# Weighing attention probabilities in fp32 on TensorE, straight from one exponential

## The reference, cut to what matters

```python
def _attn(q, k, v, scale):
    scores = jnp.einsum('bld,bmd->blm', q, k) / scale
    w = jax.nn.softmax(scores, axis=-1)
    return jnp.einsum('blm,bmd->bld', w, v)
...
ecg_out = qkv_ecg_inter + alpha * qkv_ecg_intra
pcg_out = qkv_pcg_inter + gamma * qkv_pcg_intra
...
x_norm = _ln(x, norm_g, norm_b)
xin = jnp.einsum('bsd,hd->sbh', x_norm, W_in)
def res_step(prev, xt):
    new = jnp.tanh(xt + prev @ W_res.T)
    new = LEAK * new + (1.0 - LEAK) * prev
    return (new, new)
...
gate = jax.nn.sigmoid(x @ W_gate.T + b_gate)
return reservoir_out * gate + ssm_out * (1.0 - gate)
```

## Time and profile before

| | before |
|---|---|
| median of three runs | 626.57 us |
| span of the profiled execution | 624.1 us |
| between that span and the median | 2.5 us |
| PE busy | 587.2 us, 94% |
| DVE busy | 531.1 us, 85% |
| ACT busy | 453.6 us, 73% |
| POOL busy | 191.2 us, 31% |
| granted PE clock, mean | 0.996 |

### The profile page before, as it was taken

How to read it: one execution, slowest core, us unless ns; L and a number is a source line. 1 busy time by engine, 2 the same in 40 slices (tenths; PEclk the granted TensorE clock), 3 DMA queues, 4 the chain that set the end, 5 groups by cost and what they waited for, 6 DMA issues and landing times.

```text
span 624.1 us, 28185 instructions
## 1 busy us (share of the span) xinstructions
PE 587.2 (94%) x11015; PEld 464.1 (74%) x11015; DVE 531.1 (85%) x2335; ACT 453.6 (73%) x2244; POOL 191.2 (31%) x427
## 2 busy tenths in 40 slices
PE   7887888999999999999999999999999999999973
PEld 2554454788888788888888888888799888888762
DVE  5789997899888888888898899898767788999985
ACT  4687796677777777777777777777757677777664
POOL 1545365000000000010000000000100588888886
PEclk9999999999999999999999999999999999999998
DMA  6000000000000000000000000000030000000001
GB/s 215 2 2 1 2 1 2 4 3 4 4 3 4 4 3 4 4 4 4 3 4 4 4 3 3 4 4 4 9 64 3 3 20 19 16 16 19 15 20 30
DMA packets 8629, 8.30 MB, mean 13 GB/s; under 512 B 944, under 2 KB 7088, under 8 KB 8496
## 3 DMA queue, kind: packets, MB, share of 16 engines
q1 hardware_dynamic: 8208, 5.51, 3.2%
q10 hardware_dynamic: 288, 0.99, 0.6%
HBM read 3.35 MB, written 2.10 MB: 9 GB/s over the span
## 4 chain that ended last, share of the span: by engine, by line
PE 76%; DVE 9%; issue 5%; POOL 4%; ACT 4%; DMA 1%; POOLq 0%; SPq 0%; DVEq 0%
PE PS L1454 28%; PE PS L1501 16%; PE PS L1656 6%; PE PS L1472 4%; PE PS L1466 2%; PE PS L1461 2%; PE PS L1403 2%; PE PS L1404 2%; PE PS L1410 2%; PE PS L1634 2%; PE PS L1339 2%; PE PS L1378 2%; PE PS L1362 1%; PE PS L1645 1%; PE PS L1390 1%
## 5 line engine op out<-in xcount | busy, mean ns | idle before, releaser
L613 ACT ACTIVATE y<-PS 128x16 f16<-128x16 f32 x512 | 99.0, 193 | 128.0 <-PE PS L1466 124.3
L1501 PE MATMUL PS<-ballast,ident 128*128 128x245 f16 (+6 forms) x661 | 152.0, 300 | 0.0
L1013 DVE TENSOR_TENSOR y_lo<-ys,y 128x16 f16<-128x16 f32 x512 | 98.2, 192 | 52.9 <-ACT ys L614 40.8
L1454 PEld LDWEIGHTS PS<-y,res_hi 128*128 128x128 f16 x2048 | 97.7, 96 | 52.6 <-ACT y L613 19.0
L1454 PE MATMUL PS<-y_lo,res_hi 128*128 128x8 f16 x2048 | 128.2, 168 | 0.0
L1454 PE MATMUL PS<-y,res_hi 128*128 128x8 f16 x2048 | 127.7, 168 | 0.1
L1454 PE MATMUL PS<-y,res_lo 128*128 128x8 f16 x2048 | 123.4, 166 | 0.0
L444 POOL TENSOR_TENSOR small<-small,minus_half 128x2 f32<-128x2 f32 x32 | 22.6, 706 | 304.3 <-DVE y_lo L1013 272.1
L614 ACT ACTIVATE ys<-PS 128x16 f32<-128x16 f32 x512 | 103.8, 203 | 0.0
L575 ACT ACTIVATE prob<-PS,exp_up,sc 128x512 f32<-128x512 f32 x128 | 102.3, 806 | 1.5 <-PE PS L1390 1.3
L580 ACT ACTIVATE prob_hi<-PS,exp_up,sc 128x512 f16<-128x512 f32 x128 | 103.1, 812 | 0.0
(11 more groups left out here) (225 smaller groups left out, 1368.9 us busy)
## 6 DMA issues: line engine op xcount, KB each, us to landing
ys<-in_x SPq DMA_DIRECT2D x8, 256.0 KB, 8.0
out<-gate_all SPq DMA_DIRECT2D x24, 64.0 KB, 1.5
mats<-in_mats ACTq DMA_DIRECT2D x1, 709.0 KB, 5.1
h_last<-h_all SPq DMA_DIRECT2D x4, 128.0 KB, 3.2
gate_last<-gate_all SPq DMA_DIRECT2D x4, 128.0 KB, 2.7
out<-gate_last SPq DMA_DIRECT2D x16, 32.0 KB, 1.9
rows<-in_rows ACTq DMA_DIRECT2D x1, 257.5 KB, 8.0
wall<-in_wall SPq DMA_DIRECT2D x1, 256.0 KB, 4.8
```

The costliest lines, as they stand in the source:

```text
L613: a_.activation(y16[:, :].rearrange("p (m b) -> p m b", m=NH), pre, ACT.Tanh, scale=back).then_inc(y16_ready, 1)
L1013: v.tensor_tensor(y_lo[:, :], ys[:, :, bass.ds(i * STEPS + (1 + t), 1)].rearrange("p n o -> p (n o)"), y16[:, :], ALU.subtract).then_inc(l ...
L1454: t_.matmul(dst[:, m, :], wts[:, k, m * P:m * P + P], st[:, k * B:k * B + B], start=False, stop=False, skip_group_check=True)
L1501: t_.matmul(at[:, 0:size], ident16[:, :], ballast[:, 0:size], start=False, stop=True, skip_group_check=True)
```

## The change

The probabilities stay in fp32 and the values too: one exponential for each a (`weights_of`), no high and low parts, no `low_part`, no DVE step for the values (`stack` is for queries and keys only), and no batch scale in them, so that `mix_s` goes. `weigh` takes the place of `weigh_high` and `weigh_low`: sixteen fp32 matmuls a tile with 65 columns (64 values and the ones). It is spread over seven steps by a table; the steps of other work are set anew. The fp16 low parts of the product that were left out before are now contained in the fp32 operands.

```diff
-PV = C + 2
-VW = PV + C
+PV = C + 1
...
+        WEIGHTS_AT = (8, 9, 11, 13)
+        WEIGH_AT = {10: (0, 2), 11: (2, 4), 12: (4, 6), 13: (6, 9), 14: (9, 11), 15: (11, 13), 16: (13, 16)}
...
-                g.tensor_tensor(prob_lo[:, a, :], prob[:, a, :], prob_hi[:, a, :], ALU.subtract).then_inc(prob_lo_ready, 1)
...
-                    a_.activation(v1, PS[:, n % 2, :].rearrange("p (a c) -> p a c", c=C), ACT.Identity, scale=s_col[:, b:b + 1]
-                                  ).then_inc(rounded_ready, 1)
+                    a_.activation(v1, PS[:, n % 2, :].rearrange("p (a c) -> p a c", c=C), ACT.Copy).then_inc(valued, 1)
...
-                a_.activation(prob[:, a, :], X[a], ACT.Exp, scale=e_col[:, j % B:j % B + 1], bias=exp_up[:, :])
-
-            def high_part(j, a):
-                if j > 0:
                     act.wait_ge(pv_done, (j - 1) * NA + a + 1)
-                a_.activation(prob_hi[:, a, :], X[a], ACT.Exp, scale=e_col[:, j % B:j % B + 1], bias=exp_up[:, :]).then_inc(prob_ready, 1)
+                a_.activation(prob[:, a, :], X[a], ACT.Exp, scale=e_col[:, j % B:j % B + 1], bias=exp_up[:, :]).then_inc(prob_ready, 1)
...
+                if p in WEIGHTS_AT:
+                    weights_of(j, WEIGHTS_AT.index(p))
                 if p == 22:
                     heads(j)
-                if p == (30 if j == NT - 1 else 32) and j >= AHEAD - 1:
+                if p == (31 if j == NT - 1 else 43) and j >= AHEAD - 1:
                     gate_tanh(j)
-                if p == (31 if j == NT - 1 else 35) and j >= AHEAD - 1:
+                if p == (31 if j == NT - 1 else 45) and j >= AHEAD - 1:
                     gate_half(j)
...
-                else:
-                    vals = values[:, b * NQ + 2 * (k - 2):b * NQ + 2 * (k - 2) + 2, :, :].rearrange("p n a w -> p (n a) w")
-                    v.scalar_tensor_tensor(vals[:, :, PV:VW], PS[:, n_ % 2, :].rearrange("p (a c) -> p a c", c=C), s_col[:, b:b + 1],
-                                           vals[:, :, 0:C], ALU.mult, ALU.subtract).then_inc(stacked, 1)
...
-                if p == 21:
+                if p == 16:
...
-                a = of_a(p, 10, 2)
-                if a is not None:
-                    low_part(j, a)
-                if p == 22:
+                if p == 23:
                     head_sums(j)
-                if p == 23:
+                if p == 24:
                     moments(j)
-                if p == 25:
+                if p == 26:
                     hat(j)
-                if p == 27:
+                if p == 28:
...
-            def weigh_high(j, a):
+            def weigh(j, first, last):
                 b = j % B
-                pe.wait_ge(prob_ready, j * NA + a + 1)
-                if j > 0 and a == 0:
-                    pe.wait_ge(h_ready, j)
-                if j < B:
-                    pe.wait_ge(stacked, b * 4 + 4)
-                for k in range(NQ):
-                    lhs, vals = prob_hi[:, a, k * P:k * P + P], values[:, b * NQ + k, a, :]
-                    t_.matmul(OUT[:, a, :], lhs, vals[:, 0:PV], start=a == 0 and k == 0, stop=False, skip_group_check=True)
-                    t_.matmul(OUT[:, a, 0:C], lhs, vals[:, PV:VW], start=False, stop=False, skip_group_check=True)
-
-            def weigh_low(j, a):
-                b = j % B
-                pe.wait_ge(prob_lo_ready, j * NA + a + 1)
-                for k in range(NQ):
-                    last = t_.matmul(OUT[:, a, :], prob_lo[:, a, k * P:k * P + P], values[:, b * NQ + k, a, 0:PV], start=False,
-                                     stop=a == NA - 1 and k == NQ - 1, skip_group_check=True)
-                last.then_inc(pv_done, 1)
+                for n in range(first, last):
+                    a, k = n // NQ, n % NQ
+                    if k == 0:
+                        pe.wait_ge(prob_ready, j * NA + a + 1)
+                    if n == 0 and j > 0:
+                        pe.wait_ge(h_ready, j)
+                    if n == 0 and j < B:
+                        pe.wait_ge(const_ready, 3)
+                    if n % (2 * NQ) == 0 and j < B:
+                        pe.wait_ge(valued, 2 * b + 2)
+                    one = t_.matmul(OUT[:, a, :], prob[:, a, k * P:k * P + P], values[:, b * NQ + k, a, :], start=n == 0,
+                                    stop=n == NA * NQ - 1, skip_group_check=True)
+                    if k == NQ - 1:
+                        one.then_inc(pv_done, 1)
...
-                for a in range(NA):
-                    if p == (12, 14, 15, 18)[a]:
-                        weigh_high(j, a)
-                for a in range(NA):
-                    if p == (16, 16, 19, 19)[a]:
-                        weigh_low(j, a)
-                if p == 27:
+                if p in WEIGH_AT:
+                    weigh(j, *WEIGH_AT[p])
+                if p == 28:
                     turn_hat(j)
-                if p == 29:
+                if p == (29 if j == NT - 1 else 34) and j >= AHEAD - 1:
                     gate(j)
...
-                elif r < 2 and t in (4, 5, 8, 9):
-                    fill((t - 4) // 4, (t - 1) % 2, i + 1, r + 1, 1 + r)
+                elif r < 2 and t in (2, 3, 4, 5):
+                    fill((t - 2) // 2, (t - 1) % 2, i + 1, r + 1, 1 + r)
...
-                if t in (0, 2, 3):
-                    if early and (t > 0 or i % REGIONS > 0):
-                        pad(SPARE, 240)
-                        pad(SPARE, 220)
+                tile, early, fill_at = j < NT, j <= NT, i % REGIONS < 2 and t in (2, 3, 4, 5)
+                if t in (2, 3):
+                    if early:
+                        pe.wait_ge(inv_ready, j)
+                        for n in range(1 if fill_at or t == 2 else 2):
+                            pad(SPARE, 240)
...
-                elif t in (8, 9, 10):
+                elif t in (8, 9):
                     if early:
                         pe.wait_ge(h_ready, j)
-                        for n in range(2 if fill_at else 4):
-                            pad(SPARE, 245)
-                elif tile and (t < 15 or i % REGIONS < REGIONS - 1):
-                    pe.wait_ge(prob_ready, j * NA + 1)
-                    pad(X[0], 440)
...
-                if j > 0:
-                    pe.wait_ge(gate_raw, j - 1)
-                    for n in range(4):
-                        keep_clock(MISC, 256)
                 score(j + 1, 0)
-                weigh_high(j, 0)
+                weigh(j, 0, 4)
                 score(j + 1, 1)
                 if j > 0:
                     turn_hat(j - 1)
-                weigh_high(j, 1)
+                weigh(j, 4, 8)
```

More of the change, by code:

```diff
@@ L229, in build @@
         stacked = sem("stacked")
+        valued = sem("valued")
         scored = sem("scored")
@@ L313, in tiles_at @@
                     work(p + STEPS * lag, j)
-        def of_a(p, first, step):
-            a = (p - first) // step
-            return a if 0 <= a < NA and p == first + a * step else None
+        WEIGHTS_AT = (8, 9, 11, 13)
+        WEIGH_AT = {10: (0, 2), 11: (2, 4), 12: (4, 6), 13: (6, 9), 14: (9, 11), 15: (11, 13), 16: (13, 16)}
         def half_q(c):
@@ L461, in work @@
                     gate_scale(j)
[L463 to L468, removed]
             root(0, 1, 1)
@@ L909, in sums_inverse @@
                 if j == 0:
-                    dve.wait_ge(mix_ready, 1)
+                    dve.wait_ge(mix_made, 1)
                 else:
@@ L982, in work @@
             def work(p, j):
-                a = of_a(p, 1, 1)
-                if a is not None:
-                    top_of(j, a)
+                if 1 <= p <= NA:
+                    top_of(j, p - 1)
                 if p == 5:
@@ L1007, in work @@
                     difference(j)
+                if p == (30 if j == NT - 1 else 42) and j >= AHEAD - 1:
                     gate_in(j)
@@ L1059, in steps @@
                         softplus_step(k, slice(0, FULL), sp_first, sp_first_ready)
-                if (t, i) == (5, 16):
+                if (t, i) == (13, 16):
                     dve.wait_ge(gate_raw, FULL)
-                if t == 5 and 16 <= i < 22:
+                if t == 13 and 16 <= i < 22:
                     steps(3 * (i - 16), 3 * (i - 16) + 1)
-                if t == 9 and 16 <= i < 22:
+                if t == 14 and 16 <= i < 22:
                     steps(3 * (i - 16) + 1, min(17, 3 * (i - 16) + 3))
@@ L1093, in rows_of @@
                     sigma_row(m, j, 0, P, sigma_ready, keep)
-                if B <= i < FIRST_DECAY and t in (8, 15):
-                    rows_of(i - B, (8, 15).index(t), KEPT)
+                if B <= i < FIRST_DECAY and t in (11, 15):
+                    rows_of(i - B, (11, 15).index(t), KEPT)
                 late = (2, 6, 10)
@@ L1208, in _ @@
             gate_in(AHEAD - 2)
-            for a in range(NA - 1):
-                low_part(AHEAD - 1, a)
             for i in range(FIRST_DECAY):
@@ L1335, in project @@
                     pe.wait_ge(x_loaded[b], 16)
```

(35 more changed lines are left out.)

75 lines of the change are left out of this document (18 added, 57 removed).

## The result

The changed kernel takes 804.57 us (median of five runs, 800.84 to 818.27), the kernel before 626.57 beside it: 1.284 times as long, 95% interval 1.282 to 1.286. I had forecast 654 in a range of 641 to 664. The direction was right, the size was off by 150 us. Medians here are of all executions of a kernel; its interval leaves out those more than 1.5% above the fastest.

The account below looks back on a forecast made before the run. Scan steps were taken as bound by a 0.86 us latency loop or by PE or ACT slot work, the opening by PE after the change. Scan +19.9 and opening +7.5 on 626.6 made 654 us, 8-in-10 range 641 to 664.

Parts of the forecast that it names:

- give nothing more: those steps are bound by the loop: Scan: dropped exponentials, DVE low parts, two pads in steps 11 to 15 and moved head sums bring no further change.
- Weighing matmul 0.225 us + 0.03: PE: each fp32 weighing matmul costs 0.225 us, plus 0.03 for the change of kind; 2.2 us more a tile.
- Slots: Scan, step by step: +0.68 us a plain body, +0.17 for fills, +0.85 a body; +19.9 us for the scan.
- Steps 11 and 13: Scan: gate's tanh and halving queue behind exponentials on ACT; +0.19 and +0.27 us, steps about 1.08 and 1.16.
- step 0: Scan, plain body: three fp32 matmuls replace two pads and eight low matmuls; 1.06 us against 0.89, +0.17.
- a mean body: Scan: a body of 16 steps takes about 15.2 us against 14.35.
- Step 8's pads: Scan: pads wait for head sums moved from step 6 to 7 on DVE, the scan queued behind; +0.17 us.
- Opening +7.5: Opening's nine tiles: PE becomes the bound, about 12.1 us a tile; +7.5 us in all, bounds -3 and +10.
- Last stage: Readouts after the scan: not touched by the change, 166 us as before.
- Rivals: Stalls not adding, 640 us (0.14); fp16 pace, 635 (0.04); weighing swallowed by slack, 615 (0.03); dearer weighing, 665 (0.11).

Follow-up runs that it names:

- fp16_weigh: The changed kernel with probabilities and values in fp16, same order and padding, low parts of the product left out: 694.83 us.
- pads_lean: after_pads_back without the pads of steps 0 and 10: 677.34 us.
- after_pads_back: The changed kernel with the padding of the kernel before put back in scan, opening and ninth tile: 672.7 us.
- fp16_padded: fp16_pads_back with two 500-column pads in steps 11 to 15, three of 250 in step 0, gate's tanh and halving later, head sums earlier: 613.44 us.
- after_pads_long: after_pads_back with two pads of 500 columns in place of one of 440 in steps 11 to 15: 700.58 us.
- fp16_pads_back: after_pads_back with probabilities and values in fp16, low parts of the product left out: 691.98 us.

## Why the prediction was wrong

- **The step that failed** is the assumption under all the sums, that the pads which go "give nothing more: those steps are bound by the loop", with every duration from full-clock rows and no rival on the clock. That their time was hidden fits the steps of 0.89 us before; what they gave beside it was the clock, and that term of the sum was put at nothing. Put back, they are worth 132 us. An estimate of the changed kernel at full clock is 118 to 122 (opening, below) + 24 x 15.2 + 166 + 2.5 = 651 to 655, so the forecast of 654 is about what the work costs without the loss of clock. No run has this kernel at a full clock throughout.
- **Weighing matmul 0.225 us + 0.03:** right, 0.70 for three. At the lower clock they take 0.44 each, and there the fp32 type costs 110 us in the same order (804.57 against 694.83 in fp16_weigh): the cut in padding that cost the kernel before 64 us cost this one 132.
- **Slots:** right. Steps 11 and 13 at 1.07 and 1.17; step 0 at 1.05 in pads_lean's plain bodies for 1.06; a mean body of 15.28 there for 15.2. Step 8's pads waited for the head sums as forecast, but the step takes 1.00 us in after_pads_back, +0.13 for +0.17.
- **Opening +7.5:** right as far as it can be read, though its own tiles add up to 6.5 to 7.4. In after_pads_back the first tanh comes at 124.9, 10.7 later than before. Pads that the change had dropped are part of it: 28 of 256 columns at 0.10 (2.8), and 19 of 512 at 0.21 where they lie bare (0 to 4.0). That leaves about +4 to +8, an estimate. In the changed kernel's profile it is +35, by the clock.
- **Last stage:** unchanged, as said.
- **Rivals:** none of the four had the mechanism. What spoke for it before any run: pads fill PE's slack in nearly every step of the kernel before, and the change took a dozen pads a body and two thirds of the weighing matmuls from it. The section cited of "TensorE: Matmul & The Clock Gate" is on weight loads; Part 1 of that page of the Trainium skill says that the default state is throttled and that activity releases it, and I should have weighed this. By that page idleness of PE brings the throttle back. The trace shows none, with PE's records filling 500.71 of 501.10 us at a clock of 0.54; but a record's length is not what a matmul costs, and whether PE stood idle within them no run here shows.

## What to carry to other kernels

Before costing padding at nothing because its time is hidden, ask what clock the rest would run at without it, and give the low clock a rival of its own. In this case its price is about double for pads and fp32 matmuls (0.23 to 0.44 us), in the steps without weighing too, while the fourteen short matmuls of a step stay nearly as they are. Read the granted clock by stage first: a PE that looks fully busy may have lost it. When operations are made fewer or cheaper beside a latency-bound loop, fill the slots up again, as fp16_padded does, and compare: where the clock was already full, more pads only cost (672.7 to 700.58 us in after_pads_long).

## What was not expected of the hardware

- Adding matmuls that nobody reads made a kernel faster twice: 804.57 to 672.7 us, and 691.98 to 613.44 (with ACT and DVE work moved too). Taking them out made one slower: 625.65 to 689.84.
- In one case here fp32 matmuls held the clock better than as many fp16 ones of the same shape: 0.99 against 0.66 in the same order with the same pads.
- The clock was lost in an engine that the profile shows as hardly ever idle: 500.71 of 501.10 us busy at a mean clock of 0.54.
- It comes and goes with the place in the body. Averaged over bodies 5 to 20 of the changed kernel it is 0.50 in steps 0 to 6 and 0.58 to 0.62 in steps 7 to 13; in fp16_pads_back 0.50 to 0.59 and 0.69 to 0.91.
